# Placing three layer norms of a fused two-layer decoder differently around its first FFN and at its start

## The reference, cut to what matters

```python
# block 1: RWKV time and channel mix; its first step is a layer norm with gain and bias (ln1)
tm, _ = time_mix(layernorm(x, ln1_g, ln1_b), ...)
...
x = layernorm(x + xattn0(x, ctx, mask))                     # norm1
g = x @ (w_gate.astype(f32) / 127).T                        # 256 -> 768, weights given as int32
u = x @ (w_up.astype(f32) / 127).T
x = layernorm(x + (silu(g) * u) @ (w_down / 127).T)         # norm2
# block 4: a gated linear recurrence
xn = x / max(norm(x), 1e-12) * sqrt(256) * g1               # an rms norm, rms1
lin = xn @ W_lin.T + b_lin
x_rg = lin @ W_conv.T + b_conv
...
```

## Time and profile before

| | us |
|---|---|
| median of 3 runs | 2148.8 (2146.69 to 2152.64) |
| the profiled execution | 2143.97 |
| its span, first to last instruction | 2142.1 |
| PE busy | 1815.9 (85%) |
| DVE busy | 1100.9 (51%) |
| ACT busy | 934.4 (44%) |
| POOL busy | 333.2 (16%) |
| mean granted TensorE clock | 0.94 |

### The profile page before, as it was taken

The page is one execution under the profiler, slowest core; times in us unless marked ns, Lnnn a source line. Parts: engine busy times, 40 slices in busy tenths (PEclk is TensorE's granted clock), DMA queues, the critical chain, the costliest instruction groups (busy, mean ns, idle before and its releaser), DMA issues.

```text
span 2142.1 us, 25895 instructions
## 1 busy us (share of the span) xinstructions
PE 1815.9 (85%) x7480; PEld 780.5 (36%) x7481; DVE 1100.9 (51%) x1566; ACT 934.4 (44%) x1675; POOL 333.2 (16%) x258
## 2 busy tenths in 40 slices
PE   5969969999789875868999999999997539999994
PEld 2424423222234332324333333333331416666663
DVE  4553237888231252658887687787760402222223
ACT  3242135777521224423777677677676101121221
POOL 4125011111210120331000000000001241111111
PEclk9989989999899987989999999999999569999997
DMA  6001013010100030416000000000000821111113
GB/s 237 24 32 48 0 41 103 26 30 23 56 0 0 0 104 0 50 44 128 9 9 16 9 9 16 9 9 16 1 1 25 368 75 28 27 27 28 28 28 91
DMA packets 66286, 95.21 MB, mean 44 GB/s; under 512 B 11271, under 2 KB 59975, under 8 KB 64273
## 3 DMA queue, kind: packets, MB, share of 16 engines
q1 hardware_dynamic: 59184, 84.79, 13.5%
q0 software_dynamic: 7008, 9.25, 2.6%
HBM read 63.31 MB, written 30.30 MB: 44 GB/s over the span
## 4 chain that ended last, share of the span: by engine, by line
PE 56%; DVE 6%; issue 4%; ACT 3%; POOL 3%; DMA 1%; ACTq 0%; DVEq 0%; SPq 0%; POOLq 0%
PE ps L597 9%; PE ps L1264 9%; PE ps L1939 9%; PE ps L1286 9%; PE ps L1221 8%; PE ps L1954 5%; DVE arena L1435 2%; PE ps L1585 2%; POOL rows_in L2051 1%; PE ps L1947 1%; PE ps L467 1%; PE ps L1321 1%; ACT arena L2007 1%; PE ps L1933 1%; PE ps L1272 1%
## 5 line engine op out<-in xcount | busy, mean ns | idle before, releaser
L1369 ACT ACTIVATE arena<-ps 128x512 f32<-128x512 f32 x1088 | 575.2, 600 | 205.1 <-PE ps L1286 204.4
L1435 DVE TENSOR_REDUCE arena<-ps 128x1 f32<-128x802 f32 (+1 forms) x512 | 480.5, 986 | 122.0 <-PE ps L1221 121.1
L597 PE MATMUL ps<-arena 128*128 (+1 forms) x832 | 381.6, 616 | 68.8 <-DVE arena L1737 22.8
L1286 PE MATMUL ps<-arena 100*128 100x512 bf16 x1088 | 368.9, 383 | 13.6 <-issue 5.8
L1221 PE MATMUL ps<-arena 97*128 97x401 bf16 (+2 forms) x1280 | 339.1, 347 | 31.9 <-issue 19.8
L1264 PE MATMUL ps<-arena 128*32 128x512 f32 x2176 | 290.6, 606 | 1.4 <-ACT arena L1369 1.4
L597 PEld LDWEIGHTS ps<-arena 128*128 128x128 f32 x832 | 162.7, 197 | 279.5 <-issue 275.3
L1939 PE MATMUL ps<-arena 128*128 x608 | 197.6, 468 | 29.1 <-ACT arena L2007 29.1
L1286 PEld LDWEIGHTS ps<-arena 100*128 100x128 bf16 x1088 | 104.5, 98 | 265.5 <-ACT arena L1369 187.6
L1221 PEld LDWEIGHTS ps<-arena 97*128 97x128 bf16 x1280 | 114.1, 98 | 217.6 <-DVE arena L1435 88.2
L2149 DVE TENSOR_TENSOR arena<-ps,arena 128x352 f32<-128x352 f32 x76 | 39.9, 525 | 268.1 <-ACT arena L2014 197.2
(11 more groups left out here) (204 smaller groups left out, 1470.2 us busy)
## 6 DMA issues: line engine op xcount, KB each, us to landing
arena<-in_experts_w SPq DMA_DIRECT2D x8, 2176.0 KB, 17.4
arena<-qparts SPq DMA_DIRECT2D x192, 64.0 KB, 2.3
qparts<-arena SPq DMA_DIRECT2D x48, 128.0 KB, 2.2
rows_in<-arena SPq DMA_DIRECT2D x1, 5200.0 KB, 17.7
arena<-in_ctxT SPq DMA_DIRECT2D x3, 1664.0 KB, 8.9
kparts<-arena SPq DMA_DIRECT2D x24, 208.0 KB, 2.3
arena<-kparts SPq DMA_DIRECT2D x12, 416.0 KB
arena<-rows_in SPq DMA_DIRECT2D x38, 130.0 KB, 2.0
```

What stands on the lines that cost most here:

```text
L597: ins = eng.matmul(out, w[:, k, m * P:(m + 1) * P], x[:, k, tok(c)], start=k == 0, stop=k == ktiles - 1)
L1286: eng.matmul(ring_bank(r), Kst[0:ROWS, at_head(g * HG + h), kt * P:(kt + 1) * P], Qst[0:ROWS, g, h, :], start=True, stop=True).then_inc(ri ...
L1369: eng.activation(probs[:, keys_of(u, kt) % 2, h, :], ring_bank(r), ACT.Exp, bias=0.0).then_inc(ring_read.sem, 1)
L1435: eng.tensor_reduce(MX[:, par, heads[0] * QT + q, n % 2:n % 2 + 1], got, AX.XY, ALU.max).then_inc(slot_free.sem, 1)
```

## The change

Four things are moved; nothing is taken out of the computation.

- `normalise` keeps its steps as methods of an object (`Steps`). An engine named in `woven` gets no list of its own; the caller writes its steps where it wants them.
- ln1 is called with `lag=NC`: all four chunks go through the first half of the steps on every engine, then all four through the second.
- The conversion of the FFN weights stands ahead of norm0 in POOL's list, that is ahead of the cross attention.
- norm1's last two PE steps (variance of chunks 2 and 3) stand behind slices 0 and 1 of the FFN's first chunk. norm2 and rms1 of chunk c - 1 are written into chunk c of the FFN on all four engines, with means and variances in banks 6 and 7, and the FFN is written out chunk by chunk without a loop. Behind the last chunk PE runs W_lin of the finished chunks and norm2's last two products between them.

```diff
+        ln1 = normalise("ln1", X, x_loaded, XN, lambda eng: None, vec["ln1_g"], vec["ln1_b"],
+                        lag=NC)
...
+        @part("pool")
+        def _(eng):
+            eng.wait_ge(ld_ffn, 16)
+            eng.tensor_copy(ffn_flat, ffn_int_flat).then_inc(w_float, 1)
...
+                def begin_act(self, eng):
+                    if before:
+                        before.wait_all(eng)
...
-        norm1 = normalise("norm1", X, x0_done, X, lambda eng: None, first_bank=4)
+        n1 = normalise("norm1", X, x0_done, X, lambda eng: None, first_bank=4, woven=("pe",))
...
+        n2 = normalise("norm2", X, ready_of(x_ffn), X, lambda eng: None, bank_of=lambda c: 6 + c % 2,
+                       then_rms=(XN, vec["g1"]), woven=("pool", "pe", "dve", "act"))
...
         @part("pe")
...
+            n1.begin_pe(eng)
+            for c in range(3):
+                n1.mean_product(eng, c)
+            n1.square_product(eng, 0)
+            n1.mean_product(eng, 3)
+            n1.square_product(eng, 1)
             eng.wait_ge(w_float, 1)
-            with eng.Fori(0, NC) as c:
+            n2.begin_pe(eng)
+            for c in range(NC):
                 norm1.wait(eng, c)
                 for j in range(FK):
                     if j >= 2:
                         h_done.wait(eng, c, j - 1)
                     product(eng, ps[:, 2 * (j % 2), :], ffn["gate"], j, X, c)
                     product(eng, ps[:, 2 * (j % 2) + 1, :], ffn["up"], j, X, c).then_inc(gu.sem, 1)
+                    if c == 0 and j < 2:
+                        n1.square_product(eng, 2 + j)
+                    if c > 0 and j == 1:
+                        log1.wait_all(eng)
+                        if c == 3:
+                            n2.guarded.wait(eng, 0)
+                        n2.mean_product(eng, c - 1)
+                    if c > 0 and j == 4:
+                        n2.square_product(eng, c - 1)
...
+            first_linear(0)
+            n2.mean_product(eng, NC - 1)
+            first_linear(1)
+            n2.square_product(eng, NC - 1)
+            x_ffn.wait_all(eng)
+            first_linear(2)
+            first_linear(3)
...
         @part("act")
...
+            n2.begin_act(eng)
             eng.preload_act_table_set(SILU)
...
                                    scale=DEQUANT).then_inc(silued.sem, 1)
+                    if c > 0 and j == 2:
+                        n2.square(eng, c - 1)
+                if c > 0:
+                    eng.preload_act_table_set(LN_EXP)
+                    n2.invert_root(eng, c - 1)
+                    n2.invert_rms(eng, c - 1)
+                    if c < NC - 1:
+                        eng.preload_act_table_set(SILU)
...
         @part("dve")
...
+                    if c > 0 and j == 2:
+                        n2.centre_chunk(eng, c - 1)
+                if c > 0:
+                    n2.square_mean(eng, c - 1)
+                    n2.both_scales(eng, c - 1)
                 down.wait(eng, c)
...
+        @part("pool")
...
+            for c in range(NC):
+                n2.add_halves(eng, c)
+                n2.add_squares(eng, c)
+                n2.scale_residual(eng, c)
```

More of the change, by code:

```diff
@@ L460, in _ @@
[L460 to L482, removed]
+                def scale_residual(self, eng, c):
+                    rstd.wait(eng, c)
+                    eng.tensor_tensor(dst[:, :, tok(c)], body[:, :, tok(c)], both(norm_rstd[:, tok(c)]),
+                                      ALU.mult).then_inc(scaled.sem, 1)
+                def begin_pe(self, eng):
+                    banks_free(eng)
+                    eng.wait_ge(ld_mean, 16)
@@ new lines, in mean_product, with square_product, begin_dve @@
+                def mean_product(self, eng, c):
+                    halves.wait(eng, c)
+                    eng.matmul(place(c), mean_w, norm_sum[:, tok(c)], start=True, stop=True).then_inc(mean.sem, 1)
+                def square_product(self, eng, c):
+                    squares.wait(eng, c)
+                    eng.matmul(place(c), mean_w, norm_sum[:, tok(c)], start=True, stop=True).then_inc(var.sem, 1)
+                def begin_dve(self, eng):
+                    if before:
+                        before.wait_all(eng)
+                    if early:
+                        early.all_stored(eng)
@@ L523, in both_scales, with square, invert_root @@
                                       ALU.mult).then_inc(both_inv.sem, 1)
[L524 to L547, removed]
+                    self.scale_rms(eng, c)
+                def begin_act(self, eng):
+                    if before:
+                        before.wait_all(eng)
+                    if early:
+                        early.cut.wait(eng, 4 * NC)
+                def square(self, eng, c):
                     centred.wait(eng, c) if centre else ready(eng, c)
                     eng.activation(SQ[:, :, tok(c)], body[:, :, tok(c)], ACT.Square).then_inc(squared.sem, 1)
-                def invert_root(c):
+                def invert_root(self, eng, c):
                     if centre:
@@ L1587, in _, with first_linear @@
                 ins.then_inc(down.sem, 1)
+            def first_linear(c):
+                rms1.wait(eng, c)
+                product(eng, bank(c * 2), lru["W_lin"], 0, XN, c)
+                product(eng, bank(c * 2 + 1), lru["W_lin"], 1, XN, c).then_inc(lin_mm.sem, 1)
+            n2.guarded.wait(eng, 1)
+            eng.wait_ge(ld_lru, 16)
+            first_linear(0)
[5 more added lines that the diff above has]
+            first_linear(3)
         @part("act")
         def _(eng):
+            n2.begin_act(eng)
             eng.preload_act_table_set(SILU)
-            with eng.Fori(0, NC) as c:
+            for c in range(NC):
                 for j in range(FK):
```

120 lines of the change are left out of this document (70 added, 50 removed).

## The result

Over the executions timed side by side the kernel before takes 2147.89 us (median of 4, 2146.69 to 2152.64) and the changed one 2128.55 us (median of 4, 2126.25 to 2129.65): ratio 0.9904 with an interval of 0.9887 to 0.9922, so some 20.6 us less (16.8 to 24.3). The prediction was 2126, with a range of 2116 to 2136.

The account below looks back on a forecast made before the run. PE, holding 56% of the chain, was taken to bound the kernel, so a stage is worth PE's wait in it. -7.1 - 2.35 + 5.15 - 18.6 = -22.9 from the median 2148.8 gave 2126, range 2116 to 2136.

Parts of the forecast that it names:

- ln1: At the kernel's start: all chunks abreast bring the projections from 48.39 to 41.3, -7.1 us; -5.4 if the clock falls.
- Rival 4: Behind ln1: a load or DVE's scans swallow ln1's gain, giving 2133; chance 0.05.
- The conversion: Ahead of norm0: the weights' conversion, 5.02 us, goes where POOL is idle and nobody waits, 0.
- norm1 handed over: norm1 to the FFN's first chunk: slice 2 begins 4.75 us earlier, less 2.4 of clock behind a 5.45 pause, -2.35.
- norm2 woven in: FFN chunks 1 to 3: 12 more passes at 0.43 on PE's path, +5.15 us, their chains hidden.
- rival 2: FFN chunks: woven products make PE wait, 4 us a chunk, giving back 12: 2138; chance 0.10.
- rival 5: End of chunks 1 to 3 and of the FFN: DVE and POOL hold each other up, slower at 2160; chance 0.03.
- Rival 3: FFN loop: each turn cost PE a hidden pause, 2 us a turn, so 6 more gained: 2120; chance 0.05.
- Behind the FFN: Last down product to gate products: 56.8 us become 35.8, -21.0, with +2.4 of clock for a 4.3 pause, -18.6.
- the prediction's list of signs: What would show it wrong: PE waiting at a variance product, projections later than 43, or changed stages behind W_conv.
- Rival 1: At both new pauses: the clock survives them, so 4.8 us more is gained: 2121; chance 0.14.

Follow-up runs that it names:

- e1: The kernel before with ln1's edit alone (all four chunks step by step): 2142.86 us against 2148.03, ratio 0.9974.
- e11: The changed kernel with POOL's scaling of the last chunk's residual held until DVE has scaled that chunk: 2128.30 us, ratio to before 0.9915.
- e3: The changed kernel with norm1's last two variance products back ahead of the first gate product, conversion still early: 2126.12 us, ratio to before 0.9900.
- e10: The kernel before with only the weights' conversion moved ahead of norm0 in POOL's list: 2143.89 us against 2146.61, ratio 0.9983.
- e5: The changed kernel with norm2 and rms1 back behind the FFN in their old order, FFN still written out: 2138.55 us, ratio to before 0.9962.
- e12: The changed kernel timed and traced once more, unedited: 2126.14 us, ratio to before 0.9907.
- e8: The changed kernel with W_conv products filling PE's pause behind the FFN and two W_lin biases earlier on DVE: 2119.35 us, ratio to before 0.9861.
- e9: The changed kernel with earlier norm1 variances, ACT's scaling wait moved, W_conv filling the later pause, and POOL's last residual scaling held: 2111.19 us, ratio to before 0.9822.

## Why the prediction came out right, and where it did not

**The base.** The prediction worked from one execution of before, 4.8 us below the median of its runs, and carried that difference over. The stage table says where it lay: 4.4 us between the projections and norm1, 2.6 of it by the clock at norm0's last pause. Carrying it over was right; the 2121.1 for a profiled execution was not, since that luck does not repeat: the changed kernel's two took 2129.65 and 2124.92.

**ln1, -7.1 predicted, -5.5 to -5.9 measured.** The steps came as told: four squares before the first variance, no pause in front of the early keys, the same 1.49 us at the end. Mis-sized is one term: the variances. Half of the eight passes were put at half clock (5.17 us in all); the row at 23.32 says 6.46, so nearly all of them ran at 0.50, and in the ten traces with ln1's edit they took 5.5 to 6.6. In the second pair they took 5.66, and most of the shortfall there lies in before, whose projections began at 47.25 instead of 48.39. The lower bound, -5.4, was meant for half clock in the early keys, which did not come; its size fits by accident. Rival 4 (the gain swallowed) is refuted by e1.

**The conversion, 0 predicted.** Right at its new place: nothing waits there, and the conversion takes 4.03 us beside an idle DVE, where it took 5.02 beside DVE's scalings. By the Trainium skill ("SBUF — State Buffer", section "Who interferes with whom") a DVE instruction with two SBUF inputs contends with a GpSimd instruction that reads SBUF. That cost nothing here, but e11's rows behind the FFN agree with it: 2.22 us beside POOL's scaling, 0.69 without. Wrong was the place in the sum that got its gain: it was booked under the handover.

**norm1 handed over, -2.35 predicted; -2.7 in the first pair of traces, -0.1 in the second.** Each part was near: pause 5.45 predicted and 5.36 measured, slice 2 at 24.91 us behind norm1's first mean (24.79 predicted: 606.25 less 581.46), clock lost 2.0 (2.4 predicted; 3.93 us at 0.50). The step that failed is what it was compared with. The part was priced against the kernel before, in which the conversion stood in the way, and not against the change without its handover. e3 and e10 make that comparison in the stage's traces: the conversion brings 3.3 to 5.7 us, the handover takes 3.2 back.

**norm2 woven in, +5.15 predicted, +4.69 measured.** The twelve passes cost what they should (e5: 5.16). No woven product of chunks 1 to 3 waited, so rivals 2 and 5 did not come. The difference is the loop: 0.16 to 0.19 a turn, three turns. Rival 3 had the sign right and the size (2 a turn) wrong; PE's own branches (L1573) took 0.08 to 0.24 us in the trace of before, the first at 629.2, hidden under the down product that runs until 636.94. The Trainium skill ("Runtime: NRT & Kernel Launch", section "Instruction fetch mechanics") has a taken branch stall where its target lies outside the two pages of instructions that are held; whether the loop's did, no run here shows.

**Behind the FFN, -18.6 predicted; -17.3 in the first pair, -20.0 in the second.** Pause 4.3 predicted, 4.39 measured. PE waits 0.31 us before the last variance; the sum had that wait (7.7 to 8.0), although the prediction's list of signs counts any wait at a variance product against it. What swings is the clock: behind the pause 6.24 us at 0.50 in the first trace (3.1 lost), while in e12 the 40 passes took 18.90 us instead of 20.51, and the stage of before itself took 67.34 and 68.41. Rival 1 (the clock survives) did not come. DVE's held step was foreseen, 2.22 measured where the sum took the 2.30 of the earlier trace rows, and e11 shows by 0.69 that POOL's scaling is what holds it.

**The sum.** Predicted -22.9. The two pairs of spans differ by 14.3 and 25.8, on the mean 20; the timed medians by 19.3 and, in e12, 20.5. The forecast is some 2 to 3 us too large, 1.4 of it in ln1. The four stages that it summed (ln1, norm1, the chunks, behind the FFN) differ by 21.2 and 20.9 in the two pairs, so the spread of the spans lies in the stages that it left out. Its bounds are added up wrong: the terms' own give -19.6 to -26.2, not -19.2 to -24.7.

## What to carry to other kernels

When a change has two edits at one wait, price each against the change without it: here moving 5 us of POOL work out of the way won the time, and in the traces of the stage the handover next to it gave 3 back. Work woven behind other work delays whatever hangs on it: put a product where its input arrives, not one slice later, and look for the chain (scaling, table load, Silu, bank) that starts at it. Look for products that are already possible to fill a pause of PE: here that saved the pause and the half clock behind it (e8: 6 to 8 us for a reordering), where shortening the pause (e11) brought nothing that the timed runs could tell.

## What the runs showed of the hardware that was not expected

- Two executions of one program differed by 6.8 us in span (2142.1 and 2148.9), and at norm0 the pauses were the same: what differed there was whether half clock followed, which is 2.6 of the 6.8. The same 8 passes took 3.70 us in the one and 5.33 in the other.
- ACT's wait ahead of a table load is not free: with the load behind norm1's last scaling PE paused 5.36 us, without (e5) 4.06.
- A DVE product with both inputs in SBUF took 2.22 us beside POOL's scaling of 2.35 us and 0.69 without it (e11). DVE's bias adds out of PSUM (L1593 in e9, 1.40 us for two) ran beside the same scaling at their usual length.

```profile
744.00 1.40 DVE L1593 TENSOR_SCALAR arena<-ps,arena 128x512 f32<-128x512 f32 x2
744.16 2.37 POOL L454 TENSOR_TENSOR arena<-arena 128x1024 f32<-128x1024 f32 x1 [7.51 <-DVE arena L491]
```
